# A recommendation tower on one core: the lone field's high and low parts in one tile, the groups of products divided anew

## The reference

```python
def _L0_rec_ref(inputs, w0, w1, w2, b0, b1, b2):
    x0 = inputs; xk = inputs; direct = []
    for idx, (W, b) in enumerate(params):
        z = jnp.einsum('bhd,bkd,hks->bsd', x0, xk, W) + b[None, :, None]
        z = jax.nn.relu(z)
        if idx != n_layers - 1:
            half = z.shape[1] // 2
            xk = z[:, :half, :]
            direct.append(z[:, half:, :])
        else:
            direct.append(z)
    return jnp.sum(jnp.concatenate(direct, axis=1), axis=-1)
e = jnp.stack([tbl_0[ids[:, 0]], ..., tbl_38[ids[:, 38]]], axis=1)   # 2048 x 39 x 16
z = _L0_rec_ref(e, ...)                                              # 2048 x 256
h = jnp.concatenate([z, dense_ctx], axis=1)
h = jnp.maximum(h @ W_top1 + b_top1, 0.0)
h = jnp.maximum(h @ W_top2 + b_top2, 0.0)
y = h @ W_top3
```

## Time and profile before

| what | us |
|---|---|
| median of 3 runs | 2474.45 (2474.23 to 2475.2) |
| the profiled execution, its own time | 2474.38 |
| its span, first to last instruction | 2472.6 |
| TensorE busy | 2373.9 (96%) |
| VectorE busy | 2212.4 (89%) |
| GpSimd busy | 2155.9 (87%) |
| ScalarE busy | 1364.1 (55%) |

### The profile page before, as it was taken

How to read it: one execution, slowest core, us unless ns; L and a number is a source line. 1 busy time by engine, 2 the same in 40 slices (tenths; PEclk the granted TensorE clock), 3 DMA queues, 4 the chain that set the end, 5 groups by cost and what they waited for, 6 DMA issues and landing times. The chain is left out here.

```text
span 2472.6 us, 32417 instructions
## 1 busy us (share of the span) xinstructions
PE 2373.9 (96%) x8192; PEld 1539.6 (62%) x8192; DVE 2212.4 (89%) x2047; ACT 1364.1 (55%) x1532; POOL 2155.9 (87%) x1350
## 2 busy tenths in 40 slices
PE   1799999999999999999999999999999999999999
PEld 1466666666666666666666666666666666666665
DVE  2689999999999999999999999999999999999983
ACT  2355555555555555555555555555555555555552
POOL 4799999999999999999999999999999999999640
PEclk9899999999999999999999999999999999999999
DMA  7888888888878888888888788888888878888710
GB/s 179 187 187 207 196 185 211 212 173 209 207 186 194 210 209 176 204 211 181 203 204 209 177 204 212 181 206 205 201 180 208 214 177 208 208 188 191 199 55 1
DMA packets 398547, 467.04 MB, mean 189 GB/s; under 512 B 170337, under 2 KB 179553, under 8 KB 398257
## 3 DMA queue, kind: packets, MB, share of 16 engines
q1 hardware_dynamic: 299202, 302.30, 54.3%
q10 hardware_dynamic: 78848, 159.39, 24.7%
q0 software_dynamic: 20480, 5.15, 1.8%
HBM read 457.03 MB, written 9.71 MB: 189 GB/s over the span
## 5 line engine op out<-in xcount | busy, mean ns | idle before, releaser
L458 POOL TENSOR_TENSOR low<-prod_pool,high 128x1024 fp32r<-128x1024 f32 (+1 forms) x640 | 1532.5, 2395 | 88.8 <-ACT high L775 73.2
L775 ACT ACTIVATE high<-prod_pool 128x1024 fp32r<-128x1024 f32 (+1 forms) x640 | 677.3, 1058 | 733.5 <-DVE prod_pool L516 695.9
L627 PE MATMUL z<-prod_whole,w_whole 128*128 128x512 f32 (+1 forms) x2176 | 1011.5, 594 | 5.6 <-DVE prod_whole L516 5.6
L627 PE MATMUL z<-high,w_high 128*128 128x512 f32 (+1 forms) x1920 | 939.5, 489 | 55.9 <-ACT high L775 55.9
L627 PE MATMUL z<-high,w_low 128*128 128x512 f32 (+1 forms) x1920 | 758.6, 395 | 0.0
L429 POOL DMA_INDIRECT rows<-table,index x640 | 611.5, 955 | 147.8 <-issue 99.0
L516 DVE TENSOR_TENSOR prod_whole<-xh,x 128x1024 f32<-128x1024 f32 x512 | 620.5, 1212 | 110.1 <-PE z L627 90.8
L627 PE MATMUL z<-low,w_high 128*128 128x512 f32 (+1 forms) x1920 | 614.0, 401 | 33.5 <-POOL low L458 33.3
L627 PEld LDWEIGHTS z<-prod_whole,w_whole 128*128 128x128 f32 (+1 forms) x2176 | 412.7, 190 | 355.7 <-issue 296.8
L516 DVE TENSOR_TENSOR prod_pool<-xh,x 128x1024 f32<-128x1024 f32 x512 | 621.3, 1213 | 10.0 <-POOL low L458 10.0
L627 PEld LDWEIGHTS z<-high,w_high 128*128 128x128 f32 (+1 forms) x1920 | 363.6, 189 | 229.2 <-issue 141.1
(11 more groups left out here) (45 smaller groups left out, 365.5 us busy)
## 6 DMA issues: line engine op xcount, KB each, us to landing
xh<-x_rows SPq DMA_DIRECT2D x64, 2560.0 KB, 16.5
xh<-x_rows ACTq DMA_DIRECT2D x64, 2432.0 KB, 20.6
xb<-x_rows SPq DMA_DIRECT2D x128, 546.0 KB
xb<-x_rows SPq DMA_DIRECT2D x64, 468.0 KB
xa<-x_rows SPq DMA_DIRECT2D x192, 78.0 KB
rows<-table,index POOLq DMA_INDIRECT x640
x_rows<-rows SPq DMA_DIRECT2D x256, 20.0 KB
xh<-staged SPq DMA_DIRECT2D x2, 1280.0 KB, 6.9
```

Source lines behind the costliest of these rows:

```text
L458: pool.tensor_tensor(low[0:g.rows, g.split_slot, 0:n, :], prod_pool[0:g.rows, g.slot, 0:n, :], high[0:g.rows, g.split_slot, 0:n, :].bitcas ...
L627: return pe.matmul(z[stage][:, :], weights[0:g.rows, table[stage, t], :], src[0:g.rows, i, :], start=t == 0 and weights is not w_low and s ...
L775: act.activation(high[0:g.rows, g.split_slot, 0:n, :], src[0:g.rows, 0:n, :], ACT.Copy).then_inc(high_ready, 1)
```

## The change

**The lone field.** Field 38 is loaded twice, into both halves of `xh`'s tile 19, and its weights stand in both halves of `w_high`'s tile. The group of that tile (`HALF_TILE`, kind "low parts by VectorE") is rounded by ScalarE in all 128 partitions; then VectorE overwrites the upper half of `high` with the low part. `w_low` has the weights' low part below and zeros above. TensorE needs two passes in place of three: `w_high` with both, `w_low` with both. The pads and their `memset`s go.

**The groups.** A table `GROUPS` gives kind, first tile and number of tiles. In a chunk there are 10 whole groups with 18 tiles, 9 of GpSimd's with 18, and 7 of VectorE's with 9 tiles and the two lone ones; five groups have one tile only. Stage 0 starts with its short tile. Constants such as `SUM_AFTER` stay as they are, though stages 1 and 2 now have eleven groups.

**The slots.** `places` deals the buffers over two chunks, some rounds with one slot fewer.

**First loads and index add.** For chunk 0 ScalarE copies `xa` before it issues its field load, and the field loads come in two parts, of which stage 1 awaits the first. GpSimd's index add stands at the head of the chunk's work, in front of a subtraction.

```diff
-KINDS = {
-    0: [BY_POOL, BY_DVE, BY_POOL, WHOLE],
-    1: [WHOLE, BY_POOL, WHOLE, BY_DVE, BY_POOL, WHOLE, BY_POOL, BY_DVE, BY_POOL, WHOLE],
+GROUPS = {
+    0: [(WHOLE, 6, 1), (BY_DVE, 0, 2), (BY_POOL, 2, 2), (WHOLE, 4, 2)],
+    1: [(WHOLE, 0, 2), (BY_DVE, 2, 1), (BY_POOL, 3, 2), (WHOLE, 5, 2), (BY_DVE, 7, 2), (BY_POOL, 9, 2),
+        (BY_DVE, HALF_TILE, 1), (BY_POOL, 11, 2), (WHOLE, 13, 2), (BY_DVE, 15, 2), (BY_POOL, 17, 2)],
+    2: [(WHOLE, 0, 2), (BY_POOL, 2, 2), (WHOLE, 4, 1), (BY_DVE, 5, 2), (BY_POOL, 7, 2), (WHOLE, 9, 2),
+        (BY_POOL, 11, 2), (WHOLE, 13, 2), (BY_DVE, HALF_TILE, 1), (BY_POOL, 15, 2), (WHOLE, 17, 2)],
 }
-KINDS[2] = KINDS[1]
-WHOLE_SLOTS, POOL_SLOTS, SPLIT_SLOTS = 3, 2, 5
+SLOTS = {WHOLE: 3, BY_POOL: 2, BY_DVE: 1, "split": 5}
...
+def places(n, slots):
+
+    short = next(k for k in range(n) if (n - k * (slots - 1)) % slots == 0) if n % slots else 0
+    whole = (n - short * (slots - 1)) // slots
+    assert whole >= 0 and (slots > 1 or not short)
+    rounds = whole + short
+    cut = [short * (i + 1) // rounds > short * i // rounds for i in range(rounds)]
+    return [slot for is_cut in cut for slot in range(slots - is_cut)]
...
             def chunk(c):
...
+                if ahead:
+                    make_index(ahead[0])
                 for i, (g, at) in enumerate(mine):
                     low_parts(g, at)
...
+                part = slice(H, 128) if g.half else slice(0, g.rows)
+                into = (high if g.half else low)[part, g.split_slot, 0:n, :]
                 dve.tensor_tensor(
-                    low[0:g.rows, g.split_slot, 0:n, :], prod_dve_v[0:g.rows, 0:n, :],
-                    high[0:g.rows, g.split_slot, 0:n, :].bitcast(f32), ALU.subtract,
+                    into, prod_dve_v[part, 0:n, :],
+                    high[part, g.split_slot, 0:n, :].bitcast(f32), ALU.subtract,
                 ).then_inc(low_by_dve, 1)
...
+                    elif g.half:
+
+                        wait_count(pe, made, c, g, g.of_kind + 1, g.kind)
+                        both = high[:, g.split_slot, :, :]
+                        mm(w_high, SPLIT_TILE, both, 0, True)
+                        done = mm(w_low, SPLIT_TILE, both, 0, last=True)
...
+                load_fields(sp, c, 1, xh_loaded[c.p], HALF_TILE, TK, F - 1)
...
             act.wait_ge(cols_loaded, 16)
-            load_odd_fields(0, 0)
-            copy_xa(0)
-            round_stage(0, 0)
-            layer_out(0, 0)
+            copy_xa(Chunk(0, 0))
+
+            load_first_fields(act, 1, HALF_TILE)
+            round_stage(0, Chunk(0, 0))
+            layer_out(0, Chunk(0, 0))
```

More of the change, by code:

```diff
@@ L69, with __init__ @@
 ALL_TILES = TURNED + T0
-class Group:
[L75 to L80, removed]
+KINDS = [kind for groups in GROUPS.values() for kind, _, _ in groups]
+PER = {"all": len(KINDS), "split": sum(k != WHOLE for k in KINDS),
+       **{kind: KINDS.count(kind) for kind in (WHOLE, BY_POOL, BY_DVE)}}
+def places(n, slots):
[5 more added lines that the diff above has]
+    return [slot for is_cut in cut for slot in range(slots - is_cut)]
+PLACES = {kind: places(2 * PER[kind], slots) for kind, slots in SLOTS.items()}
+class Group:
+    def __init__(self, stage, chunk, g, counts, users):
+        of = GROUPS[stage]
+        self.stage, self.chunk, self.g = stage, chunk, g
+        self.kind, first, n = of[g]
+        self.tiles = range(first, first + n)
+        self.begins_layer, self.ends_layer = g == 0, g == len(of) - 1
+        self.half = stage > 0 and first == HALF_TILE
+        self.rows = 128 if stage else (LAST0 if first == T0 - 1 else JT * F)
         self.split = self.kind != WHOLE
@@ L98, in plan, with __init__, __add__, __sub__ @@
         order += [(1, c)] + [(0, c + 1)] * (c + 1 < CHUNKS) + [(2, c)]
-    return {(stage, c): [Group(stage, c, g, counts) for g in range(len(KINDS[stage]))]
+    return {(stage, c): [Group(stage, c, g, counts, users) for g in range(len(GROUPS[stage]))]
             for stage, c in order}
 PLAN = plan()
-EVERY = [g for gs in PLAN.values() for g in gs]
-SPLITS = [g for g in EVERY if g.split]
-WHOLES = [g for g in EVERY if not g.split]
 LIKE = 2
[L109 to L114, removed]
+class Chunk:
+    def __init__(self, n, like):
+        self.n, self.like = n, like
+        self.known = isinstance(n, int)
+        self.p = like % 2
+    def __add__(self, k):
+        if self.known:
+            return Chunk(self.n + k, self.n + k)
+        return Chunk(self.n + k, LIKE + (self.like + k) % 2)
+    def __sub__(self, k):
+        return self + -k
 WHOLE_TILE, SPLIT_TILE = {}, {}
@@ L266, in groups @@
         def groups(stage, c):
-            return PLAN[stage, c if isinstance(c, int) else LIKE + (stage == 0)]
+            return PLAN[stage, c.like]
         def count(c, group, value, per):
-            if isinstance(c, int):
+            if c.known:
                 return value
-            return (c - group.chunk) * PER[per] + value
+            return (c.n - group.chunk) * PER[per] + value
         def wait_count(engine, semaphore, c, group, value, per):
@@ L350, in load_pairs, with store_feats @@
                     sp.dma_start(xb[at, 0:n, :], shifted).then_inc(x0_loaded, 16)
[L352 to L369, removed]
+            def store_feats(c):
+                sp.wait_ge(direct_summed, c.n + 1)
+                sp.wait_ge(last_summed, c.n + 1)
+                sp.dma_start(feats_dram[:, :, bass.ds(c.n * CB, CB)],
+                             chunk_feats[c.p][:, :, :]).then_inc(feats_stored[c.p], 16)
```

314 lines of the change are left out of this document (173 added, 141 removed).

## The result

The changed kernel takes 2450.19 us (median of four runs, 2449.59 to 2451.98), the kernel before 2474.82 (also four runs): a ratio of 0.9902 with a 95% interval of 0.9884 to 0.9919. It is faster, by 24.6 us where 49.5 was forecast, and lies just above the predicted range. The profiled execution took 2451.98, its span is 2450.1.

The account below looks back on a forecast made before the run. GpSimd bounded the kernel at 36.18 us per chunk; afterwards VectorE's loop, 35.45, just above TensorE's 35.3. 61 x (36.18 - 35.45) = 44.5, plus 4.7 and 0.3, is 49.5 off 2474.38: 2424.9 us, range 2406 to 2450.

Parts of the forecast that it names:

- The gather that went with it stays: GpSimd, steady chunk: one of ten groups goes, ten gathers stay over nine; 33.1 us, so 2 us of rest.
- VectorE's legs, 14.1, 15.8 and 5.5: VectorE's walk through stage 2, stage 1 and stage 0 of a steady chunk, in us; together a loop of 35.45.
- The half low part's starts, 0.11 each: VectorE, stage 1: the half low part and what follows it start without overlap, 0.11 us each, 0.22 together.
- TensorE's own work, 35.3: TensorE's passes per steady chunk take 35.3 us, 0.3 less than before; as bounding rival 2409 us, chance 0.22.
- the third loop, 35.3: From stage 2's start through GpSimd's low parts there, TensorE and stage 1 to VectorE's next stage 2: 35.3 us.
- its 0.82 is covered: GpSimd, each chunk: the 0.82 us lost behind the index add is hidden by standing ahead of a subtraction.
- Buffers, loads in steady chunks: Steady chunks: slots dealt over two chunks and the lone field's second fetch cost nothing; xb load likewise if landing in 21.5 us.
- slower rival: Each chunk: xb lands after ScalarE wants it, stopping three roundings; chunk 37.25 us, kernel 2534 us; chance 0.04.
- Start, -4.7: Start of the kernel: 4.7 us less, 2 from the first loads and 2.7 from one low part fewer in chunk 0.
- Alone, 1.8 MB is 8 us: Start: first loads without the odd fields' load beside them take 8 us at 225 GB/s; chunk 0 up to 12 earlier.
- hardly moves: Start: ScalarE's second copy of xa, at 83.44 us before, stays about there, so only 2 us of gain is kept.
- The three loops add up: Rival: stage 2's low parts come a little late each time, after a double gather or late relu; 35.9 per chunk, 2452 us; chance 0.2.

Follow-up runs that it names:

- first experiment: Changed kernel with the second gather moved from behind the chunk's first GpSimd low part to behind its fifth (stage 0's): 2438.13 us, ratio 0.9853.
- The kernel with 35.30: Changed kernel with the second gather behind the fifth low part and the lone tile's low part made in all 128 partitions: 2421.78 us, single run.

## Why the prediction was wrong, step by step

- *GpSimd: "The gather that went with it stays", "has 2 us of rest".* This step failed, and it is the largest part of the miss. GpSimd does rest, 2.6 in the chunk, so the sum was about right; but a sum over a chunk says nothing of where the rest lies. The walk was made for GpSimd's low parts in stage 2, with one gather behind each, and never for those of stage 1, where the tenth gather stands behind the first of three low parts, and TensorE waits for the third. Its place is in the loop: 1.22 (4.75 from that low part to the next, 1233.49 to 1238.24, instead of 3.53). The three runs with the gather in three places show it. It costs 0.18 per chunk over the whole run (35.76 against 35.58), 11 us.
- *VectorE's legs, 14.1, 15.8 and 5.5.* Right. With the gather out of the way (first experiment) they are 14.12, 15.87 and 5.58. So 35.45 was low by 0.13, 8 us: 0.08 of it in stage 0, the rest in stage 1 and in rounding. As a bound the step held, once the gather was moved.
- *The half low part's starts, 0.11 each.* Right in place and size. The half low part and the instruction behind it, in stage 1 and in stage 2, begin 0.03 behind the end of their forerunner, where most other starts overlap it by 0.08; 1226.71 and 1227.44 above are one pair. Without them, and only when VectorE bounds, a chunk is 0.27 shorter, where 0.22 was in the sum. By the rule that the prediction took from the Trainium skill (VectorE: DVE Perf Modes, Two Vector instructions with no wait between them), a start in another quadrant of partitions is held until the earlier instructions have finished. The trace agrees, and it shows one more such start, which the prediction did not count: in stage 2 the product behind the sum (1228.15) also begins 0.02 behind, and overlaps again in the run without the half low part. The sum reads no PSUM and this product does, but no run takes that cause by itself. It hides under the relus like the pair in front of it.
- *TensorE's own work, 35.3, and the third loop, 35.3.* Neither was reached by the changed kernel. With one gather more in it the third loop is 36.43; less that gather's 1.22 this is 35.2, an estimate that bears the 35.3 out. The kernel with 35.30 comes to both, so no run here shows whether TensorE could go lower.
- *The index add, "its 0.82 is covered".* Right, and worth more than was seen: alone it takes the chunk from 36.18 to 35.79.
- *Buffers, loads in steady chunks.* Right: ScalarE's wait for xb appears twice, both in the start, and the slower rival with it is out.
- *Start, -4.7.* Wrong in sign: +5.2. It was put together from 2 for the first loads and 2.7 for the gathers, and the first part failed: chunk 0's stage 2 starts 7.6 later (100.13 against 92.53), not 2 earlier. "Alone, 1.8 MB is 8 us": the first copy stood at 41.27, 16.6 behind the first xb issue at 24.70, and not near 32; in the eight profiled executions with the new first loads it came 14.7 to 16.6 behind that issue. The copy of chunk 1's xa, put at "hardly moves", stood at 88.73 instead of 83.44, since chunk 1's loads, which await the store of its rows, went out at 64.65 instead of 59.65. With the old first loads in the changed kernel they went out at 60.84 and the copy stood at 84.47. And behind that copy stand three roundings instead of one: from the copy to stage 2 it is 11.40 where it was 9.09. Of these 7.6, then, 5.3 come ahead of the copy and 2.3 behind it. Why that store landed 5.0 later is not shown beyond this. The other part, fewer low parts over chunk 0's twenty gathers, held: from chunk 0's to chunk 1's stage 2 it is 42.05 now and was 44.41, 2.4 less where 2.7 was expected.
- *The rivals.* "The three loops add up" gave 35.9 and 2452, next to the measured 35.79 and 2450. Its mechanism, a double gather ahead of a low part, was the right one, but placed in stage 2; the run that puts it there gives 36.43. It should have been walked through instead of given a chance of 0.2.

The misses add: 11 us for the gather, 8 for the legs, 10 for the start (from -4.7 to +5.2), less 1.5 that the end gave beyond its 0.3 (0.7 and 1.1 above), are 27.5; the forecast's 49.5 less the 22.5 of the spans is 27.

## What to carry to other kernels

Rest on an engine is worth something only in the loop that ends last: walk each of the loops in which work of that engine stands, and put extra issues behind the piece of work that nobody awaits before the next rest. When a copy is moved ahead of others, count what queues behind it in the one place where its load is late, the start, and not in the steady state alone. Do the smallest part of a change by itself: moving the index add here gave all that the whole change did.

## What was unexpected of the hardware

- The same instructions up to chunk 0's stage 2 put its start anywhere from 95.87 to 100.13 in executions of three kernels that differ only behind it (the changed kernel 100.13, the gather moved 98.60, the gather in stage 2 95.87), and the first copy of xa at 41.27, 38.34 and 37.86. A single execution can't settle a few microseconds of the start.
- The first xb load took 14.7 to 16.6 us from its issue with one field load fewer beside it, and 22.3 before, 21.9 with the old first loads in the changed kernel: taking that transfer away gave 5 to 8 us, not the 14 that the mean rate of the queue had suggested.
- VectorE's hold at a change of partitions costs 0.11 and is paid twice for a single instruction, on its start and on that of the next (1.24 and 0.73 where it is 1.13 and 0.60 without). In stage 2, where the sum stands behind it, a third start is held.
